# Second attention: the second head's last, widest tile of each pair divided on ScalarE instead of GpSimd

## The reference, cut to what matters

```python
EMB, NQ, NKV, D = 128, 16, 4, 64
q = _rotary((x @ Wq + bq).reshape(b, s, NQ, D))
k = _rotary((x @ Wk + bk).reshape(b, s, NKV, D))
v = (x @ Wv + bv).reshape(b, s, NKV, D)
logits = jnp.einsum('bqhgd,bkhd->bhgqk', qg, k) * scale
logits = jnp.where(causal, logits, jnp.float32(-1e+30))
w = jax.nn.softmax(logits, axis=-1)
out = jnp.einsum('bhgqk,bkhd->bqhgd', w, v).reshape(b, s, NQ * D)
return out @ Wo + bo
```

## Time and profile before

| | |
|---|---|
| median of three runs | 1482.98 us |
| lowest, highest | 1474.93, 1483.29 us |
| the profiled execution | 1472.26 us, of which 1470.5 from the first instruction to the last (the span) |
| granted TensorE clock, mean over the span | 0.86 of full speed |
| busy: TensorE, its weight load, VectorE, ScalarE, GpSimd | 1177.6, 566.5, 800.8, 648.2, 466.3 us |

### The profile page before, as it was taken

The page is one execution under the profiler, slowest core; times in us unless marked ns, Lnnn a source line. Parts: engine busy times, 40 slices in busy tenths (PEclk is TensorE's granted clock), DMA queues, the critical chain, the costliest instruction groups (busy, mean ns, idle before and its releaser), DMA issues. The chain is left out here.

```text
span 1470.5 us, 18597 instructions
## 1 busy us (share of the span) xinstructions
PE 1177.6 (80%) x6601; PEld 566.5 (39%) x6601; DVE 800.8 (54%) x1852; ACT 648.2 (44%) x1456; POOL 466.3 (32%) x495
## 2 busy tenths in 40 slices
PE   2788545888978769899878769899978688989686
PEld 1112121222444424344445424344445455455454
DVE  4677327683865476563865376663875322666212
ACT  1267312675355226665355226666255223255122
POOL 2000024000869040000869040000779030399000
PEclk6579655788999769999989769999989789999799
DMA  5600030000002000000002000000000000000000
GB/s 147 155 2 2 8 86 0 2 1 2 1 8 75 12 1 2 2 2 8 1 8 72 15 1 1 2 2 8 1 1 1 1 0 1 8 1 1 1 0 8
DMA packets 28811, 23.88 MB, mean 16 GB/s; under 512 B 12264, under 2 KB 25648, under 8 KB 27952
## 3 DMA queue, kind: packets, MB, share of 16 engines
q1 hardware_dynamic: 28720, 22.70, 5.9%
HBM read 14.96 MB, written 7.34 MB: 15 GB/s over the span
## 5 line engine op out<-in xcount | busy, mean ns | idle before, releaser
L701 DVE TENSOR_REDUCE mx<-ps 128x1 f32<-128x512 f32 x512 | 324.0, 683 | 179.6 <-PE ps L1149 177.8
L927 ACT ACTIVATE PROB<-ps 128x512 f32<-128x512 f32 x512 | 274.2, 602 | 203.2 <-PE ps L1140 202.4
L428 POOL TENSOR_SCALAR PROB<-PROB,rsum 128x128 f32<-128x128 f32 (+3 forms) x256 | 277.7, 1102 | 43.6 <-DVE rsum L803 43.2
L969 ACT ACTIVATE PROB<-ps,mx 128x128 f32<-128x128 f32 (+3 forms) x256 | 132.9, 524 | 190.4 <-DVE mx L798 187.3
L1149 PE MATMUL ps<-kst,qst 24*128 24x512 bf16 x512 | 157.3, 455 | 49.5 <-DVE mx L701 26.4
L891 ACT ACTIVATE MREG<-ps,b_sb 128x512 f32<-128x512 f32 x128 | 88.1, 689 | 180.6 <-PE ps L1077 180.0
L1171 PE MATMUL ps<-PROB,v 128*32 128x512 f32 x1024 | 162.0, 713 | 3.7 <-ACT OREG L936 2.4
L798 DVE TENSOR_REDUCE mx<-ps 128x1 f32<-128x128 f32 (+3 forms) x256 | 113.1, 484 | 93.7 <-PE ps L1215 93.4
L1229 PE MATMUL ps<-cst,PROB 128*128 128x128 f32 x640 | 111.2, 296 | 59.6 <-POOL PROB L428 23.4
L1077 PE MATMUL ps<-xnT,w_sb 128*128 128x512 f32 x256 | 148.7, 683 | 10.1 <-DVE MREG L646 5.6
L1140 PE MATMUL ps<-qst,kst 27*128 27x512 bf16 x512 | 131.0, 418 | 27.1 <-ACT PROB L927 15.2
(11 more groups left out here) (178 smaller groups left out, 1302.9 us busy)
## 6 DMA issues: line engine op xcount, KB each, us to landing
qk_terms<-RREG SPq DMA_DIRECT2D x48, 128.0 KB, 2.1
kst<-qk_terms SPq DMA_DIRECT2D x16, 192.0 KB
qst<-qk_terms SPq DMA_DIRECT2D x16, 192.0 KB
w_sb<-in_L_ffn_W_dram SPq DMA_DIRECT2D x1, 2048.0 KB
qst<-mrow SPq DMA_DIRECT2D x96, 4.0 KB
XN<-in_L_attn_x_dram SPq DMA_DIRECT2D x4, 256.0 KB, 2.9
out_dram<-XP SPq DMA_DIRECT2D x4, 256.0 KB, 2.3
wq_sb<-in_L_attn_Wq_dram SPq DMA_DIRECT2D x1, 512.0 KB, 4.9
```

Source lines behind the costliest of these rows:

```text
L428: pool.tensor_scalar(tile, tile, rsum1[:, 2 * v + half:2 * v + half + 1], None, ALU.mult).then_inc(scaled1, 1)
L701: dve.tensor_reduce(mx0[:, ga % 2, col:col + 1], ps[:, max_banks[MAX_SLOT[n] % len(max_banks)], :], AX, ALU.max, negate=True).then_inc(slo ...
L927: act.activation(prob0[:, s % 2, q % 4, q % 8 // 4], ps[:, s0_banks[q % len(s0_banks)], :], ACT.Exp, scale=float(HD0) ** -0.5).then_inc(ex ...
L969: act.activation(prob1[:, half, at:at + w], ps[:, a1_bank(v, half), 0:w], ACT.Exp, bias=mx1[:, col:col + 1], accum_out=sum1[:, col:col + 1 ...
```

## The change

On GpSimd, `scale_probs` leaves out the second head's tile in every fourth step (qt = 3). ScalarE gets it, as `scale_last(v)`: in step v + 1, after the Exps of tile v + 1 and ahead of the copy of the turned tile. It multiplies in place with an ACTIVATE of the Copy function, whose scale is the column of reciprocals, and counts on a semaphore of its own. TensorE's waits are renumbered: 7 divisions of a pair come from GpSimd and one from ScalarE. The number of divisions stays 256, of which 32 are moved, 8 in each run.

```diff
@@ gpsimd, scale_probs
-                for half in range(2):
+                for half in range(1 if v % 4 == 3 else 2):
                     tile = prob1[:, half, P * (v % 4) * (v % 4 + 1) // 2:][:, 0:w]
                     pool.tensor_scalar(tile, tile, rsum1[:, 2 * v + half:2 * v + half + 1], None, ALU.mult).then_inc(scaled1, 1)
@@ scalar, attention1
+                def scale_last(v):
+
+                    act.wait_ge(rcp1_ready, NV * r + v + 1)
+                    tile = prob1[:, 1, 6 * P:10 * P]
+                    act.activation(tile, tile, ACT.Copy, scale=rsum1[:, 2 * v + 1:2 * v + 2]).then_inc(scaled1_act, 1)
...
                 for v in range(V_FIRST):
                     probabilities(v)
+                    if v == 4:
+                        scale_last(3)
...
                 for v in range(V_FIRST, V_END):
                     if v < NV:
                         probabilities(v)
+                    if v > 4 and v % 4 == 0 and v <= NV:
+                        scale_last(v - 1)
                     if v - TURN_LAG < NV:
                         keep_turned(v - TURN_LAG)
                     turn(k, nx, v)
@@ tensor, turn_probs
                     for i, kept in enumerate((kept1_dve, kept1_act)):
-                        pe.wait_ge(scaled1, 2 * (NV * r + u) + i + 1)
+                        if i == 1 and qt == 3:
+                            pe.wait_ge(scaled1_act, 8 * r + u // 4 + 1)
+                        else:
+                            pe.wait_ge(scaled1, 7 * (8 * r + u // 4) + 2 * qt + i + 1)
```

More of the change, by code:

```diff
@@ L263, in build @@
         a1_ready, max1_done, exp1_done, rcp1_ready = sem("a1_ready"), sem("max1_done"), sem("exp1_done"), sem("rcp1_ready")
-        scaled1, turned1, kept1_dve, kept1_act = sem("scaled1"), sem("turned1"), sem("kept1_dve"), sem("kept1_act")
+        scaled1, scaled1_act = sem("scaled1"), sem("scaled1_act")
+        turned1, kept1_dve, kept1_act = sem("turned1"), sem("kept1_dve"), sem("kept1_act")
         av1_done, oT_ready = sem("av1_done"), sem("oT_ready")
```

## The result

The changed kernel takes **1456.99 us**, the median of four runs (1451.96 to 1459.74); the kernel before, on the same chip and beside it, 1482.42 (1474.93 to 1483.29). The ratio on record is 0.984, with an interval of 0.9805 to 0.9875 (the two medians alone divide to 0.983): 1.6% faster, and quicker than the 1472 that was forecast and than the low end of 1459. The profiled execution took 1456.04 us, with a span of 1454.2 and a mean granted clock of 0.862 (before 1472.26, 1470.5, 0.86).

The account below looks back on a forecast made before the run. TensorE is busy 80% of the span, with GpSimd's division the heaviest chain line. Gains of 4.0, 4.0, 2.1 and 0.7 us in the four runs made -10.8, from the median 1472 us; range 1468 to 1477, down to 1459, up to 1484.

Parts of the forecast that it names:

- period 9.27 for 9.28: Fourth run, regular pair of heads' tiles: forecast 9.28 us where it was 8.92, set by ScalarE and no longer GpSimd.
- no table load: ScalarE's new ACTIVATE: no load counted; one of 1.283 us in each of 32 places and back would be +82 us.
- the two last turns together: End of each run: the second head's last turn should follow the first's by 0.46 us, not 1.54.
- the sum had -0.7: Fourth run of the second attention: gains and losses of its pairs and end summed to -0.7 us.
- the backlog: GpSimd's queued work in the second halves of the first and second run; its shift and the ends give -4.0 us each.
- -10.8 us, before the clock: Total over the four runs of the second attention: -4.0 - 4.0 - 2.1 - 0.7, without TensorE's clock.
- the third run's -2.1: Third run: the 2.78 us wait shrinks by 1.15, a late copy returns 0.12, the end brings 1.08.
- the end, -1.08 in each run: Last tiles of each run: GpSimd has three tiles instead of four, so the second head's turn comes 1.08 us sooner.
- Until 440 nothing moves: First and second run, first half: no change, as TensorE waits for VectorE's other work in any case.
- All waits for GpSimd go: Rival: ScalarE's scaling hides, regular period 8.72 us, about -17 us, 1466 us; chance 0.27.
- The gain is eaten: Rival: reciprocals hold GpSimd back in the second halves, only the ends' gains remain: 0 us, 1483; chance 0.18.
- Slower: Rival: scaling of 1.0 us or more delays the copy, +14 us, 1497; with table loads 1565; chance of either 0.05.

Follow-up runs that it names:

- fill_ends: Kernel before, with TensorE given seven and six identity transposes in two pauses at each run's end, GpSimd and ScalarE untouched: 1466.91 us, ratio 0.9911.
- ends_only: Kernel before, with only the last tile of each run (v = 31), four in all, divided on ScalarE: 1467.56 us, ratio 0.9904.
- early_only: Kernel before, with only tiles v = 3 and v = 15 of the first three runs, six in all, divided on ScalarE: 1478.6 us, ratio 0.9996.
- copy_first_r3: Changed kernel, with ScalarE's copy of the turned tile ahead of the scaling in the fourth run only: 1452.47 us, ratio 0.9826.
- before_fourth: Kernel before, unchanged, one more execution for a fourth trace: 1485.17 us, mean clock 0.850.
- best_filled: Changed kernel, with the copy first in the fourth run and 18 identity transposes in step 18's pause of the first three runs: 1445.36 us, ratio 0.9778.
- copy_first: Changed kernel, with the scaling on ScalarE placed behind the copy of the turned tile in all runs: 1453.8 us, ratio 0.9831.
- extra_on_act: Kernel before, GpSimd dividing everything, plus 32 ACTIVATEs of the same form on ScalarE into a scratch tile: 1475.08 us, ratio 0.9981.
- before_again: Kernel before, unchanged, run again for the spread and a second trace: 1479.39 us, ratio 1.0012.

## Why the prediction failed

**Where the mechanism was right.** In the fourth run each step came as written: period 9.27 for 9.28, ACTIVATE 0.719 for 0.69, no table load, the copy as the releaser with a wait of 0.37, no wait ahead of the 512-wide turn, the two last turns together. To the last values this run moved -1.0 us (70.2 to 69.2) where the sum had -0.7. Two errors partly cancel there, and that is luck: four regular pairs lose 0.35, not three, and the last stretch, from the seventh pair's values to the eighth's, gains 1.78 us (8.62 to 6.84), not 1.0; some 0.5 of it is the clock, since fill_ends gets that much there with GpSimd untouched. In the first and second run the backlog moved as I had it: from the fourth pair's values to the last ones it is 43.4 us in all four traces of before and 39.1 in both of the changed kernel, -4.3 for -4.0. Up to the last values the first run has -4.0 (mean 91.4, from 90.3 to 92.1, to 87.4) and the second, whose four traces agree, -4.9 (92.3 to 87.4).

**The step that failed is "-10.8 us, before the clock".** I left TensorE's clock out of the sum, though my own traces had 4.49 us for 16 matmuls that take 2.37 elsewhere. The changed kernel takes away one of the three short pauses (1.00, 0.88 and 0.72 us) behind which TensorE fell, and shortens another. From the last values to the projection the four runs take 17.3 us before (mean of four traces: 4.0, 4.9, 3.2 and 5.3; their sum is 16.4 to 18.2) and 12.6 after: -4.7 us. In the third run, from the turn that waited 2.78 us to the next values it is 8.94 us before (1117.25 to 1126.19) and 7.55 after (1106.17 to 1113.72), although TensorE waits longer for GpSimd in that stretch after than before (0.46 and 0.67 us, for 0.21): 1.4 us for the lower level. With it the third run's -2.1 becomes -3.5, of -4.4 (88.5 to 84.1, and the same in all). With the 0.5 at the fourth run's end the clock makes 6.6 of the 8.2 us that the four runs gained beyond my sum. fill_ends shows that the end's part is the clock and not the shorter wait: with GpSimd as slow as ever, the same 4.7 and 0.5 us go, and the median falls by 12.1. The term "the end, -1.08 in each run" is the one that was mis-sized most: -4.3 in the sum; in the changed kernel the last stretch gains 1.3, 1.3, 1.1 and 1.8 us and what follows the last values another 4.7, together -10.2, and ends_only has -11.5 in the median.

**"Until 440 nothing moves" failed too**, for a smaller amount. I looked at TensorE's waits there and found VectorE ahead of them, but not that VectorE itself was held by GpSimd. Its L726 takes 0.80 us beside GpSimd's L434 and 0.40 after; its four tiles at L601 took 1.65 beside two 512-wide tiles of GpSimd, and 1.27 beside the one that is left. That puts 0.4 us at the start and about 0.4 near step 15 into each of three runs. early_only shows both in its trace, and 0.4 to 0.5 of them left at the last values of its second and third run, but its total doesn't show them. In the changed kernel the second run is 0.9 beyond my sum by the last values, and the third, with 1.4 for the clock, 0.9 (-4.4 for -3.5): of that size. That these are the same us is argued, not shown.

**The rivals.** "All waits for GpSimd go" is false: the regular period is 9.27 us and not its 8.72, and TensorE still waits for it in the first run of the changed kernel, 3.8 us of the 6.4. Who waited for whom there, 440 to 481 us (total, times, longest):

```profile
PE ps L1243 <- POOL PROB L429: 3.8, 4, 1.8
```

The time that it named, 1466, is nearer to the measured one than mine, for a reason that did not happen. "The gain is eaten" is false as well: the second halves kept their 4 us. "Slower" is false by its price, 0.719 us against the 1.2 or so from which it decides, but its mechanism is real in the fourth run, where it takes 3.3 us that copy_first_r3 gets back.

**The sizes.** The spread of 8 us between three runs was too small a base for the range: 17 runs of before reach over 18 us, and the low end of 1459 is itself 1 us above what its own sum gives (1474.93 less 17). What spreads the runs goes with the missing term: the quickest of the 17, 1468.32, has a mean granted clock of 0.862 and the slowest, 1486.28, one of 0.850.

**What stays open.** The four runs account for -19.0 us. The medians differ by 24 to 25. The other 5 to 6 us would be outside the runs, where before_fourth is 12.6 us longer than the first trace and the changed kernel's two are only 2 and 4 longer; fill_ends likewise has 6.2 us in its runs and 12.1 in its median. I can't say from these traces why an execution stays at the lower level there. The kernels with the ends changed vary by 3 to 10 us (best_filled least, copy_first most), but over 4 to 6 executions each; the two without (early_only, extra_on_act) vary by 11 to 13 over 12, as before does by 15. That the ends set what happens between the runs is not shown.

## What to carry to other kernels

When the engine that bounds a kernel shows the same instructions at two durations, price the pauses ahead of the slow ones too: here filling pauses of 0.7 to 0.9 us with thirteen idle transposes at the end of each run gave 12.1 us in the median (5.2 of them seen as clock in the trace's runs), and filling one of 2.4 us gave 2.5 each time. Look at a moved instruction's place in the order: in the fourth run the same ACTIVATE cost 3.3 us ahead of a copy and nothing behind it, while the second and third run were 1.6 and 0.7 us longer in the one trace with it behind. And compare kernels by the stretches that the change touches, since the rest of the program can differ by over 12 us between two executions of one kernel.

## What the hardware did that I had not expected

- The same pauses don't always cost the same. TensorE at the end of the first run, in the profiled execution of before and then in before_again:

```profile
478.19 0.66 PE L1229 MATMUL ps<-cst,PROB 128*128 128x128 f32 x4 [0.99 <-POOL PROB L428]
479.73 0.66 PE L1229 MATMUL ps<-cst,PROB 128*128 128x128 f32 x4 [0.88 <-POOL PROB L428]
481.11 2.37 PE L1239 MATMUL ps<-PROB,MREG 128*64 128x512 f32 x16 [0.72 <-issue]
```

```profile
478.65 0.66 PE L1229 MATMUL ps<-cst,PROB 128*128 128x128 f32 x4 [0.99 <-POOL PROB L428]
480.19 0.66 PE L1229 MATMUL ps<-cst,PROB 128*128 128x128 f32 x4 [0.88 <-POOL PROB L428]
481.57 4.07 PE L1239 MATMUL ps<-PROB,MREG 128*64 128x512 f32 x16 [0.72 <-issue]
```

  Pauses of 0.99, 0.88 and 0.72 us in both, the values at the higher level in one and at the lower in the other. In the second and fourth run all four traces of before have them at the lower, in the third none has.
- VectorE beside GpSimd. One 128x64 TENSOR_SCALAR out of SBUF takes 0.255 us with GpSimd idle, 0.39 to 0.41 beside a 0.6 us instruction of GpSimd's and 0.78 to 0.80 beside one of 1.28; each time it ended 0.04 to 0.07 us after GpSimd's. The Trainium skill, "SBUF — State Buffer", section "Who interferes with whom", says that VectorE in its 2-port mode and GpSimd hold a shared pair of ports for a whole instruction, and the other blocks. L726 fits this. L601 doesn't quite: the tile that began at 427.45 in the kernel before took 0.70 us (0.34 alone) and ended at 428.15, while GpSimd's second tile ran from 427.37 to 428.96; and the next tile took 0.33 us, all of it beside that same tile of GpSimd's. There VectorE was neither blocked for GpSimd's whole instruction nor slowed throughout.
